# Query and key transposes of a transformer block: from TensorE to transposing transfers, in fp16 halves

## The reference

```python
h = tok(x)                               # softmax(q^T k) v, per batch element
h = h + attn(layernorm(h))
h = h + ffn(layernorm(h))

# attn: q, k, v = x @ Wq.T, x @ Wk.T, x @ Wv.T
q = rms_norm(q, qn_w)                    # y * rsqrt(mean(y * y) + eps) * (1 + w), per head
k = rms_norm(k, kn_w)
q = q * cos + rotate_half(q) * sin       # rotary embedding, by position
k = k * cos + rotate_half(k) * sin
scores = einsum('bhgtd,bhkd->bhgtk', q * 128 ** -0.5, k)
scores = where((dist >= 0) & (dist <= 128), scores, lowest)
out = softmax(scores) @ v @ Wo.T

# ffn: weights rounded to -1, 0 or 1
out = (sigmoid(x @ w1.T) * (x @ w2.T)) @ w3.T
```

## Time and profile before

| | |
|---|---|
| median of 3 runs | 1106.71 us (1106.57 to 1110.37) |
| the profiled execution, its own time | 1115.52 us |
| its span, first to last instruction | 1113.7 us |
| TensorE's mean granted clock, share of full speed | 0.956 |
| busy: TensorE, VectorE, GpSimd, ScalarE | 1022.4, 713.8, 539.8, 440.5 us |

### The profile page before, as it was taken

One profiled execution on the slowest core, in us unless ns is written; L12 is line 12 of the kernel. 1 busy time (PEld: TensorE's weight loads), 2 busy tenths in 40 slices (PEclk: granted clock), 3 DMA queues, 4 the chain that ended last, 5 costly groups with the idle time before them and its releaser, 6 DMA issues.

```text
span 1113.7 us, 20347 instructions
## 1 busy us (share of the span) xinstructions
PE 1022.4 (92%) x7783; PEld 562.2 (50%) x7783; DVE 713.8 (64%) x1267; ACT 440.5 (40%) x761; POOL 539.8 (48%) x432
## 2 busy tenths in 40 slices
PE   4989889898877599999999999999999999999996
PEld 2433333333322237657466475574765746647554
DVE  6767666778785756557656575575655765657542
ACT  1777675567663423314133232231321313314121
POOL 2576665366688744515435245253451543524500
PEclk9999898889988689999999999999999999999998
DMA  8978785665523001010101001011001010100000
GB/s 236 270 258 253 240 247 164 187 197 179 173 82 100 19 19 30 19 38 19 38 28 28 28 19 38 28 28 38 28 19 38 19 38 28 29 28 19 29 11 20
DMA packets 70436, 92.05 MB, mean 83 GB/s; under 512 B 39296, under 2 KB 39936, under 8 KB 70400
## 3 DMA queue, kind: packets, MB, share of 16 engines
q1 hardware_dynamic: 70400, 91.60, 28.1%
...
## 4 chain that ended last, share of the span: by engine, by line
PE 71%; DVE 9%; issue 7%; POOL 5%; DMA 4%; ACT 2%; SPq 1%; POOLq 0%; DVEq 0%; ACTq 0%
PE ffn_sum L1236 7%; PE ffn_sum L1237 7%; PE proj L1302 5%; PE proj L1303 5%; PE proj L1304 5%; PE tok_out L652 4%; PE score_rows L627 4%; PE proj L1190 3%; PE proj L1192 3%; PE proj L1191 3%; PE score_cols L642 3%; DVE row_max L475 3%; PE transposed L1184 3%; DVE ctx_lo L1090 2%; DMA q_parts<-max_lo 2%
## 5 line engine op out<-in xcount | busy, mean ns | idle before, releaser
L936 POOL TENSOR_TENSOR roped<-rope_cos,rope_sin 128x512 f32<-128x512 f32 x80 | 102.3, 1278 | 230.5 <-DVE rope_sin L1059 230.5
L475 DVE TENSOR_REDUCE row_max<-score_rows 128x1 f32<-128x512 f32 x256 | 163.4, 678 | 57.5 <-PE score_rows L627 57.3
L435 ACT ACTIVATE exps<-score_cols 128x512 f32<-128x512 f32 x256 | 139.6, 601 | 88.0 <-PE score_cols L642 87.0
L1236 PE MATMUL ffn_sum<-x_hi,ffn_w 128*128 128x128 f16 x1408 | 167.1, 220 | 7.7 <-DMA x_lo<-x_lo_rows 7.7
L1237 PE MATMUL ffn_sum<-x_lo,ffn_w 128*128 128x128 f16 x1408 | 166.9, 220 | 0.0
L627 PE MATMUL score_rows<-k_parts,q_parts 96*128 96x512 f32 x256 | 123.5, 497 | 26.2 <-DMA k_parts<-qk_split 14.2
L1236 PEld LDWEIGHTS ffn_sum<-x_hi,ffn_w 128*128 128x128 f16 x1408 | 138.2, 98 | 12.9 <-DMA x_lo<-x_lo_rows 8.2
L1237 PEld LDWEIGHTS ffn_sum<-x_lo,ffn_w 128*128 128x128 f16 x1408 | 138.6, 98 | 2.3
L642 PE MATMUL score_cols<-q_parts,k_parts 98*128 98x512 f32 x256 | 111.2, 443 | 16.5 <-DMA q_parts<-max_lo 11.5
L627 PEld LDWEIGHTS score_rows<-k_parts,q_parts 96*128 96x128 f32 x256 | 53.2, 209 | 119.7 <-DVE row_max L475 62.7
L379 POOL TENSOR_TENSOR exp_sums<-exps 128x512 f32<-128x512 f32 x64 | 82.1, 1313 | 58.7 <-PE score_rows L627 36.2
...
## 6 DMA issues: line engine op xcount, KB each, us to landing
...
```

The costliest lines, as they stand in the source:

```text
L435: nc.scalar.activation(E[:, n % NE, :], ST[n % 3][:, :], ACT.Exp, scale=TOK_SCALE).then_inc(exp_done, 1)
L475: nc.vector.reduce_max(row_max[:, g % 2, k:k + 1], S[n % NS][:, :], AX.X).then_inc(s_free, 1)
L1236: nc.tensor.matmul(dst, w, x2h[:, k, :], start=(k == 0), stop=False)
```

## The change

K and Q are no longer turned by TensorE. ScalarE casts the rotated rows of each chunk to fp16 (rope_high, roped_hi_rows), GpSimd subtracts (rope_low, roped_lo_rows), and SyncE sends ten transposing transfers a tile (turn_high, turn_low) into k_hi, k_lo, q_hi, q_lo. So that the halves stay in fp16's range, the rotary tables are scaled by powers of two when they are set up. K is multiplied by its inverse norms as before; Q's sixteen inverse norms per row are taken in one power (inv_rms_q) and multiplied onto the transposed scores by VectorE. The scores are three passes of fp16 matmuls, 48 in all. On TensorE, all gate products now stand ahead of the scores, all 22 down products behind them and ahead of the next tile's K. The work of the other engines is reordered to match.

```diff
@@ -744,16 +745,20 @@
...
+        self.rope_hr = sb("roped_hi_rows", [P, 1 + KV, D], F16)
+        self.rope_lr = sb("roped_lo_rows", [P, 1 + KV, D], F16)
...
+        self.kh, self.kl = (sb(name, [P, KV, P], F16) for name in ("k_hi", "k_lo"))
+        self.qh, self.ql = (sb(name, [P, KV, G, P], F16) for name in ("q_hi", "q_lo"))
...
@@ -799,10 +805,34 @@
...
+        dve.wait_ge(self.gain_set, 7)
+        dve.wait_ge(self.const_set, 2)
+        for m, power in ((0, Q_SHIFT), (1, K_SHIFT)):
+            nc.vector.tensor_scalar(tables[:, 2 * m:2 * m + 2, :], tables[:, 2 * m:2 * m + 2, :], gain[:, m:m + 1],
+                                    2.0 ** power, ALU.mult, ALU.mult).then_inc(self.const_set, 1)
...
@@ -904,9 +933,27 @@
...
+            def turn_high(n, c):
+                sp.wait_ge(r_hi, 5 * n + c + 1)
+                if c == 0:
+                    sp.wait_ge(scored, n)
+                    sp.dma_start(kh[:, :, :], rope_hr[:, c, :], transpose=True).then_inc(k_turned, DMA)
+                else:
+                    sp.wait_ge(scored, n)
+                    sp.dma_start(qh[:, c - 1, :, :], rope_hr[:, c, :], transpose=True).then_inc(q_turned, DMA)
+
+            def turn_low(n, c):
+                sp.wait_ge(r_lo, 5 * n + c + 1)
+                if c == 0:
+                    sp.dma_start(kl[:, :, :], rope_lr[:, c, :], transpose=True).then_inc(k_turned, DMA)
+                else:
+                    sp.dma_start(ql[:, c - 1, :, :], rope_lr[:, c, :], transpose=True).then_inc(q_turned, DMA)
...
@@ -917,14 +964,32 @@
...
-                if ffn:
-                    turn_x2(n - 1)
+                if attn:
+                    turn_high(n, 1)
+                if ffn:
+                    turn_x2_high(n - 1)
+                if attn:
+                    turn_low(n, 1)
+                if ffn:
+                    turn_x2_low(n - 1)
+                if attn:
+                    turn_high(n, 2)
+                    turn_low(n, 2)
+                    turn_high(n, 3)
+                    turn_high(n, 4)
+                    turn_low(n, 3)
+                    turn_low(n, 4)
                 if more:
                     rows1.turn(sp, n + 1)
                 if ffn:
                     sp.wait_ge(o_out, n + START)
                     sp.dma_start(out[bass.ds((n - 1) * P, P), :], o_tile[:, :]).then_inc(out_done, DMA)
-
+                if more:
+                    turn_high(n + 1, 0)
+                    turn_low(n + 1, 0)
...
@@ -934,21 +999,40 @@
...
-                pool.wait_ge(mean_sq, 5 * n + c + 1)
-                of = slice(G * c, G * c + G)
-                nc.gpsimd.tensor_tensor(rr[:, of], ms[:, of], minus_half[:, 0:G], ALU.pow).then_inc(rms, 1)
-                pool.wait_ge(added, 5 * n + c + 1)
-                pool.wait_ge(rms, 5 * n + c + 1)
-                view = rope[:, c, :].rearrange("p (h d) -> p h d", d=HD)
-                nc.gpsimd.tensor_tensor(view, view, bcast(rr[:, of], [P, G, HD], 2), ALU.mult).then_inc(q_ready, 1)
+
+            def scale_k(n):
+                pool.wait_ge(mean_sq, 5 * n + 1)
+                nc.gpsimd.tensor_tensor(rr[:, 0:G], ms[:, 0:G], minus_half[:, 0:G], ALU.pow).then_inc(rms, 1)
+                pool.wait_ge(added, 5 * n + 1)
+                pool.wait_ge(rms, n + 1)
+                view = rope[:, 0, :].rearrange("p (h d) -> p h d", d=HD)
+                nc.gpsimd.tensor_tensor(view, view, bcast(rr[:, 0:G], [P, G, HD], 2), ALU.mult).then_inc(k_ready, 1)
+
+            def rope_low(n, c):
+                pool.wait_ge(r_hi, 5 * n + c + 1)
+                nc.gpsimd.tensor_tensor(rope_lr[:, c, :], rope[:, c, :], rope_hr[:, c, :], ALU.subtract
+                                        ).then_inc(r_lo, 1)
+
+            def inv_rms_q(n):
+                pool.wait_ge(mean_sq, 5 * n + 5)
+                nc.gpsimd.tensor_tensor(rr[:, G:], ms[:, G:], minus_half[:, :], ALU.pow).then_inc(rms_q, 1)
 
             rope_sum(0, 0)
+            scale_k(0)
+            rope_low(0, 0)
 
             def body(n, attn, ffn):
                 if not attn:
                     return
-                for c in range(1, 1 + KV):
-                    rope_sum(n, c)
+                rope_sum(n, 1)
+                rope_low(n, 1)
+                rope_sum(n, 2)
+                rope_low(n, 2)
+                rope_sum(n, 3)
+                rope_sum(n, 4)
+                rope_low(n, 3)
+                rope_low(n, 4)
+                inv_rms_q(n)
...
@@ -956,6 +1040,8 @@
...
+                    scale_k(n + 1)
+                    rope_low(n + 1, 0)
...
@@ -983,48 +1069,53 @@
...
+                    square(n, 2)
+                    rope_high(n, 1)
...
-                    for c in range(2, KV + 1):
-                        square(n, c)
+                    square(n, 3)
+                    square(n, 4)
+                    rope_high(n, 2)
                     act.wait_ge(proj, NPROJ * (n + 1))
                     nc.scalar.mul(v[:, :], BANK[NPROJ - 1][:, :], V_SHIFT).then_inc(v_out, 1)
+                    rope_high(n, 3)
+                if ffn:
+                    tanh(n - 1, 0)
+                if attn:
+                    rope_high(n, 4)
...
@@ -1120,38 +1214,36 @@
...
+                    hidden_lo(n - 1, 1)
+                    gate(n - 1, 2)
...
                     nc.vector.transpose(sm[:, :, :].rearrange("p u k -> p (u k)"), SCORES[:, :]).then_inc(taken, 1)
-                if ffn:
-                    hidden_lo(n - 1, 1)
-                if attn:
                     dve.wait_ge(taken, n + 1)
+                    dve.wait_ge(rms_q, n + 1)
+                    link(nc.vector.tensor_tensor(sm[:, :, :], sm[:, :, :], bcast(rr[:, G:], [P, HEADS, SEQ], 2), ALU.mult))
+                if ffn:
+                    hidden_lo(n - 1, 2)
...
-                    gate(n - 1, 2)
...
-                    hidden_lo(n - 1, 2)
...
@@ -1226,6 +1312,9 @@
...
+                if f == 1 and m == 0 and not (isinstance(n, int) and n + 1 >= NTT):
+                    pe.wait_ge(squared, 5 * (n + 1) + 3)
+                    pe.wait_ge(roped_b, 5 * (n + 1) + 3)
...
@@ -1237,31 +1326,22 @@
...
+                pe.wait_ge(v_out, n + 1)
+                pe.wait_ge(k_turned, 2 * DMA * (n + 1))
+                pe.wait_ge(q_turned, 2 * KV * DMA * (n + 1))
                 for h in range(KV):
-                    for b in range(BT):
-                        ins = nc.tensor.matmul(SCORES[b * SEQ:(b + 1) * SEQ, h * P:(h + 1) * P],
-                                               kT[:, h, b * SEQ:(b + 1) * SEQ], qT[:, h, b * P:(b + 1) * P],
-                                               start=True, stop=True)
+                    for i, (k_part, q_part) in enumerate(((kh, qh), (kl, qh), (kh, ql))):
+                        for b in range(BT):
+                            of = slice(b * SEQ, (b + 1) * SEQ)
+                            ins = nc.tensor.matmul(
+                                SCORES[of, h * P:(h + 1) * P].rearrange("p (g t) -> p g t", g=G), k_part[:, h, of],
+                                q_part[:, h, :, of], start=(i == 0), stop=(i == 2))
...
@@ -1312,23 +1392,18 @@
...
                         project(n, c)
 
-                for f in range(NF):
-                    for m in range(2):
-                        if ffn:
+                if ffn:
+                    for f in range(NF):
+                        for m in range(2):
                             gate_products(n - 1, f, m)
-                        if attn:
-                            for c in TRANSPOSE_AT.get((f, m), []):
-                                transpose_qk(n, c, ffn)
-                            if (f, m) == SCORES_AT:
-                                scores(n)
-                if ffn:
-                    down_products(n - 1, range(0, DOWN_FIRST))
+                if attn:
+                    scores(n)
+                if ffn:
+                    down_products(n - 1, range(KF))
                 if attn and not last:
                     project(n + 1, 0)
                 if attn:
                     weigh_values(n, ffn)
-                if ffn:
-                    down_products(n - 1, range(DOWN_FIRST, KF))
                 if attn:
                     output_products(n)
...
```

113 lines of the change are left out of this document (58 added, 55 removed).

## The result

The changed kernel takes 1197.9 us (median of four runs, 1192.0 to 1202.0) against 1108.5 us before: a ratio of 1.079, 95% interval 1.076 to 1.083. The forecast was 1169 us in a range of 1130 to 1202 us: the side and the range hold, the point is 29 us too low.

What follows compares the result with a forecast made beforehand. TensorE, 92% busy, was taken as the bound. Per tile -1.65 + 3.02 + 0.4 + 0.2 = +2.0 us, with the clock +4.2; 14 tiles +58.8, with the end tiles +63: 1106.7 to 1169 us, range 1130 to 1202.

Steps and rivals of the forecast that it cites:

- The bound: Steady loop: a tile costs TensorE's work plus its few waits; period before the change 45.35 us.
- (D): GpSimd's 16-wide power costs 4.3 us, so rstd, xn and the score transpose come late: 1192 us; chance 0.07.
- (A): The forecast case: bare chain before the output products and clock loss, 1150 to 1185 us; chance 0.50.
- (C): SyncE's transposing transfers bind too, q's last half some 2 us late: 1197 us, or 1205 and more; chance 0.17.
- The uncovered stretch: Before the output products: fourteen down products move away, +3.02 us a tile, leaving a 3.4 us idle stretch on TensorE.
- The clock: At the output products: granted clock falls after the new idle stretch, +2.2 us a tile, between 1.65 and 2.9.
- (B): The clock stays up after the idle stretch: 1137 us, or 1123 with scores at 0.67 us; chance 0.17.
- The softmax chain: From scores' end to values' products: chain 7.8 us against 7.34 of cover, so TensorE waits some 0.4 us.
- TensorE's own work: Transposes removed 2.20 us, old score passes removed 1.10, 48 half score matmuls added 1.65: net -1.65 us a tile.
- The transfers: SyncE's ten more transfers a tile: x2's low half +0.2 us (0 to 1), last query chunk in time.
- (E): Faster: only TensorE's work counts, copies behind the values' products fit into 1.47 us: 1080 us; chance 0.05.
- (F): Gains and stalls cancel within half a per cent; chance 0.04.

Runs made afterwards that it cites:

- e9: Kernel before, with only its 22 down products all moved ahead of the values' products, nothing left between these and the output products: 1192.3 us, ratio 1.074.
- e3: Changed kernel with the down products in two lots again, 8 before the values' products and 14 between them and the output products: 1182.0 us, ratio 1.068.
- e2: Changed kernel plus 14 spare matmuls, results unread, in TensorE's idle stretch before the output products of full tiles: 1162.8 us, ratio 1.049.
- e11: Changed kernel with the next tile's rstd ahead of the 16-wide power and 7 spare matmuls before the output products: 1131.1 us, ratio 1.019.
- e1: Changed kernel with the next tile's rstd moved ahead of the 16-wide power on GpSimd: 1151.2 us, ratio 1.040.
- e4: Changed kernel's transfers and half passes, with the old order around them (scores ahead of gate group 2, down products split) and rstd ahead of the wide power: 1132.7 us.

## Why the prediction was right, and where it was 29 us short

**The bound.** That a tile costs what TensorE does plus its waits held: the ledger closes within 0.04 us. Of the signs of being right, the idle stretch, the clock (0.93) and the missing transposes came; the period, 51.2 us, did not (49 to 50). Of the signs of being wrong, (D)'s came: VectorE waits for rstd ahead of xn. The time also lies outside (A)'s own 1150 to 1185 us. It is inside the wide range, by 4 us, only because that range reached up for (C) and (D), together 0.24: (C) didn't happen and (D) did in part. That the range just held is luck.

**The uncovered stretch** (+3.02 and a bare chain of 4.49 us): right to the hundredth (795.58 to 800.07). e9 shows it alone, 3.1 us of idle time on the old kernel. What the term left unsaid is that it is a trade: where the cover went, it had been needed as well. e3 gives it back and gains none of it.

**The clock** (+2.2, bounds 1.65 to 2.9): measured 2.37, and e2 shows it as a cause, not only beside the idle time. Rival (B), the clock staying up, falls for this stretch. That the point came so near is in part luck: stretches of the same length cost 1.4 to 2.8 us in the loops of three kernels, and tile 0, which the bound of 2.9 rests on, lost nothing in e9's trace.

The Trainium skill's rule on gaps between bursts (TensorE: Matmul & The Clock Gate, Why this matters for your kernels) held against this change. It speaks of long gaps only, and e11's 1.69 us, which cost nothing, agree with it; e9's tile 0, where 3.43 us cost nothing, shows that a gap doesn't always bring the clock down.

**The softmax chain** (+0.4): this is the step that failed, by 2.2 us a tile or 31 us in all. Its own length was right (7.58 us against 7.68). Wrong was the time at which it could start: "rstd ends at 20.9 us, as before". Two things went wrong there. The first is the price, 1.6 us for the 16-wide power, which takes 2.92. The reading "the one-wide at 742.27 took 1.07 too, so most of it is fixed cost" took one row for the 1-wide power. In the trace after, 1-wide powers take 0.55 us and 4-wide ones 1.02, so the width does cost: 0.16 us for each column more, from 1 to 4 and from 4 to 16. The trace of before had both: seventeen 1-wide powers at 0.55 us with no VectorE instruction beside them, and fourteen at 1.05 to 1.10 us, each beside a hidden_lo. The two rstd of one tile, and what stood beside the second:

```profile
724.95 0.55 POOL L822 TENSOR_TENSOR rstd<-var,minus_half 128x1 f32<-128x1 f32 x1 [7.19 <-DVE var L817]
...
742.24 0.69 DVE L1082 SCALAR_TENSOR_TENSOR hidden_lo<-x2n_tanh_hidden,hidden_hi 128x512 f16<-128x512 f32 x1 [1.39 <-ACT hidden_hi L983]
```

The second is that VectorE had no time to spare behind xn, which the forecast put at nothing. Even a power of 1.6 us from 780.79 would have let rstd end only at some 782.9, with VectorE ready for xn at 781.90: some 1.0 us late, an estimate from these rows, of which the 0.24 us that e1 shows at the transpose would have hidden little. Price and place had both been looked at, as rival (D), with 0.07: at 4.3 us it gave 1192 us. The mechanism of (D) is what happened, at two thirds of its price. But (D)'s own sum, with rstd at 23.6 us and the transpose 1.5 to 2 us late, leaves 0.1 to 0.6 us for a power of 2.92, where rstd ended at 22.6 us and the transpose came 2.4 us late: it left out the waits and the longer hidden_lo behind xn, and counted the scores 0.8 us too dear.

e1 shows the rest: without the power ahead of it the wait is 0.2 us.

**TensorE's own work** (-1.65): 0.8 us too dear. 48 half passes took 0.87 us from the last gate matmul's slot to the first down product: four on the four strips of output rows start together and the groups follow each other by 0.056 us, as 784.71 and 784.77 above. The lower bound, 0.67, was the near one; the row of fp32 score passes that I took instead holds for fp32. The Trainium skill's rule on packing (the same page, Part 3, Packing small matmuls), with its estimate of 0.7 us, agrees with the trace.

**The sum.** Waits +2.2, scores -0.8 and clock +0.2 leave 1.6 us a tile, or 23 of the 29 us. Two more are the kernel before, whose median with one run more is 1108.5 us and not 1106.7. The last 4 were not traced to a place. They aren't between the first tile's addition of the residual and the last's: there the two traces differ by 84.1 us, 82.2 in the fourteen tiles and 1.9 in the last, for which +3.5 was forecast (its terms as written add up to 4.1). So it is rather 5 to 6 us that stay open, outside that stretch.

**The transfers** (rival (C)): x2's low half is 0.22 us late, as forecast. The last half of q leaves SyncE's queue at 783.1 and is there in time for scores at 784.71. (C) didn't happen, but e4 shows how near it stood: with the old place of the scores they wait 2.25 us.

**Rivals (E) and (F)** fall with the 3.31 us of idle time in every tile.
